# A graph-network kernel whose second layer changes its order of blocks, with a reordered start

## The chip, the cores and the metric

The kernel runs on one core of a Trainium2 chip. The metric is the device time of one execution in microseconds. A profile is one further execution, recorded by the chip's profiler; its span is the time from its first to its last instruction.

## The reference

Two graph layers over 6250 nodes and 200000 edges, all features 128 wide, the edges sorted by receiver `dst`. Cut to what matters:

```python
h = x @ W + b_W; xi, xj = split(h, 2)
m = xj[src] + (edge_attr @ W_e + b_We)
x = layernorm(x + xi + segment_sum(m / (deg[dst] + 1e-6), dst))     # layer 1
h = x @ W1                                                           # layer 2
deg = segment_sum(1, [dst, self]); dinv = rsqrt(deg)
o = segment_sum(h[src] * dinv[src] * dinv[dst], [dst, self]) + b     # with self loops
y = leaky((o - mean) * rsqrt(var + 1e-5) * gamma + beta)             # batch norm over nodes
return layernorm(x + y)
```

## The kernel before

**Blocks and counts.** Receivers are taken in 25 blocks of 256 nodes (the last has 106). For each block the kernel builds a dense matrix of counts, senders by receivers: how many edges run from each sender to each receiver of the block. It is made in 16 slots of 8 pairs of receivers. In each slot VectorE makes two tiles of one-hots (`one_hots`, L509 and L512), TensorE multiplies them (`count`, L737) and ScalarE copies the result to `counts` (`pair_out`, L929). TensorE then gathers by matmuls: `product` (L758) sums x over senders, x being kept as two f16 halves (`xsplit`), so 50 groups of 128 senders make 100 passes of 256 columns.

**The order in one block.** All engines run through blocks b = 0 to 26 and slots s = 0 to 15 in program order. In block b the counts of b are built, the product of b-1 runs, and block u = b-2 gets its end of the first layer: `messages` (sums times weights, s = 1), `offset` and `sums` (VectorE), `root` (ScalarE), `normalise` (VectorE), `z_out` (ScalarE), `z_low` (VectorE). What comes out is z, layer 2's input scaled by 1/sqrt(deg), again as two f16 halves in `zown`. Features of edges are summed by matmuls with one-hots of 32 receivers: `edges` (L777), 2 groups of 4 sets of `EJ` = 10 tiles of 128 edges each, with `edge_one_hots` (L529) from VectorE and 640 KB loads by SyncE.

**The own part of x.** x times (wi + identity) plus a bias is made for all nodes during block 0: `turn_x` (TensorE, 13 groups of transposes), `x_turned` (ScalarE), `own_product` (TensorE, L852), `add_bias` (VectorE, L576). The result lies in the memory that z takes later; `offset` (L583) reads it.

**Starting.** `heads` are every 125th receiver, 1600 numbers, spread to all partitions; VectorE counts in them, GpSimd fetches rows and edges by indirect DMA, and so the start of each block is found. Ahead of block 0 VectorE also prepares the weights (L626 to L630), takes the largest |x| of each row (`largest`, L536) and makes from it a power of two (`scales`) by which x is scaled when it is split (`split_high` on ScalarE, `split_low` on VectorE).

**The second layer.** Block k's product of z can take the senders whose z is ready while the first layer still runs: `early(k)` = 4(k-1) of the 100 passes are made in the first layer (L766) and stored to DRAM. The counts from that point on are stored too (`counts_kept`), except for blocks 23 and 24, which stay in SBUF. After the first layer the blocks are taken in the order `AGAIN`: 0, 23, 24, 1, 2, ..., 22. For the i-th:

- SyncE (in one queue, in this order for each i): `load_counts(i)` (L316) waits for the buffer, gathered i-4; `load_early(i)` (L323) waits for the sums of i-2; `load_inverse(i)` (L329) waits until i-2 is scaled. There are four buffers of counts.
- TensorE: `gather_z(i)` (L818), the 100 - early passes; after the first 20 of them `weights(i-1)` (L835); at the end `add_own(i)` (L827), four matmuls of the block's own z with an identity, for the self loops.
- VectorE: `add_early(i+1)` (L702), then `scale_rows(i)` (L710), then statistics (L695) after ScalarE's bias (`bias_rows`, L1058).

```python
for i in range(NB):                              # VectorE
    if i + 1 < NB and early(AGAIN[i + 1]):
        add_early(i + 1)
    scale_rows(i)
for i in range(1, NB):                           # SyncE
    if i >= 4:
        load_counts(i)
    if early(AGAIN[i]):
        load_early(i)
    if i >= 2:
        load_inverse(i)                          # reach(sp, S["scaled"], i - 1)
```

Last come the batch norm, leaky and the second layer norm (`finish_rows`, lines from L1056 on).

## Time and profile before

| what | value |
|---|---|
| time, median of 3 runs | 1067.37 us (1064.99 to 1072.68) |
| the profiled execution: its time, its span | 1061.45 us, 1059.7 us |
| busy: TensorE, VectorE, ScalarE, GpSimd | 939.2, 700.0, 474.3, 301.6 us |
| mean granted TensorE clock | 0.974 |
| DMA | 249.12 MB, 235 GB/s |

The profile records one execution. "Busy" is the time in which an engine had an instruction in work; PEld is TensorE's weight load, which overlaps PE. In a row of the timeline, what stands in brackets is the engine's idle time before the instruction and what ended it. "SPq" is SyncE's queue issuing a DMA. A span can be cut into stretches, to see which engine is busy in which.

### The profile page before, as it was taken

The numbers are of one execution on the slowest core, as the hardware profiler recorded it, in microseconds if no ns is written. First come the engines' busy times: TensorE is split into PE (matmuls) and PEld (weight loads), VectorE is DVE, ScalarE is ACT, GpSimd is POOL, SyncE is SP. The second block draws the span as 40 slices with busy tenths as digits, with TensorE's granted clock in tenths as the row PEclk, the third lists the DMA queues.
The fourth block names the chain that finished last, engine by engine and source line by source line (L and its number), as shares of the span: only waits on it lengthen the run. The fifth ranks groups of instructions, "written<-read, shape, count | busy, mean of one in ns | idle before, by whom it ended". The sixth has DMA issues, their size and how long they took to land. (4 is left out here: it accounts for less than half of the span.)

```text
span 1059.7 us, 32142 instructions
## 1 busy us (share of the span) xinstructions
PE 939.2 (89%) x12860; PEld 837.3 (79%) x12860; DVE 700.0 (66%) x1728; ACT 474.3 (45%) x932; POOL 301.6 (28%) x389
## 2 busy tenths in 40 slices
PE   2378999998999999999999999999999989887755
PEld 0377888887988988899889888899888778675655
DVE  3978999998998898888888787787511010111256
ACT  1445666665665565565555455455521000000037
POOL 4325655554554333332333323132000000000000
PEclk9899999999999999999999999999999999998878
DMA  7527989899687878787777666666036667665534
GB/s 149 209 106 251 337 328 377 317 350 345 233 321 251 316 249 282 262 283 254 223 243 224 202 227 227 196 193 203 35 153 242 266 240 280 227 217 189 149 102 148
DMA packets 95714, 249.12 MB, mean 235 GB/s; under 512 B 41156, under 2 KB 63384, under 8 KB 90696
## 3 DMA queue, kind: packets, MB, share of 16 engines
q1 hardware_dynamic: 93160, 242.12, 66.3%
q0 software_dynamic: 2400, 4.88, 1.6%
q8 instruction: 104, 1.70, 0.7%
q14 instruction: 50, 0.41, 0.1%
HBM read 192.50 MB, written 54.46 MB: 233 GB/s over the span
## 5 line engine op out<-in xcount | busy, mean ns | idle before, releaser
L929 ACT CAST counts<-pair_ps 128x800 bf16<-128x800 f32 x391 | 319.2, 830 | 301.5 <-PE pair_ps L737 286.9
L509 DVE TENSOR_TENSOR lo_oh<-counter,lo_t 128x1024 bf16<-128x1024 bf16 x391 | 273.5, 700 | 91.3 <-PE pair_ps L737 85.7
L758 PE MATMUL x_ps<-counts,xsplit 128*128 128x256 bf16 (+1 forms) x2500 | 312.6, 271 | 5.9 <-issue 5.8
L758 PEld LDWEIGHTS x_ps<-counts,xsplit 128*128 128x128 f16 x2500 | 227.6, 98 | 37.1 <-issue 14.5
L512 DVE TENSOR_TENSOR key_oh<-counter,key_t 128x800 bf16<-128x800 bf16 x391 | 226.5, 579 | 0.0
L737 PE MATMUL pair_ps<-key_oh,lo_oh 128*128 128x100 bf16 x3128 | 207.0, 208 | 18.6 <-ACT counts L929 6.4
L737 PEld LDWEIGHTS pair_ps<-key_oh,lo_oh 128*128 128x128 bf16 x3128 | 181.7, 98 | 33.1 <-issue 16.2
L766 PE MATMUL x_ps<-counts,zown 128*128 128x256 bf16 (+1 forms) x1104 | 131.5, 268 | 0.0
L777 PE MATMUL e_ps<-streams 128*32 128x128 f32 x3920 | 120.5, 276 | 1.6 <-issue 1.5
L702 DVE TENSOR_TENSOR s_mem<-pair_ps,early_in 128x256 f32<-128x256 f32 (+1 forms) x23 | 9.6, 418 | 160.0 <-PE pair_ps L827 160.0
L777 PEld LDWEIGHTS e_ps<-streams 128*32 128x32 f32 x3920 | 106.3, 111 | 6.8 <-issue 2.7
L766 PEld LDWEIGHTS x_ps<-counts,zown 128*128 128x128 f16 x1104 | 99.8, 98 | 12.4 <-issue 2.6
L818 PE MATMUL pair_ps<-streams,zown 128*128 128x256 bf16 x796 | 93.8, 278 | 17.2 <-DMA streams<-counts_kept 17.2
L818 PEld LDWEIGHTS pair_ps<-streams,zown 128*128 128x128 f16 x796 | 78.8, 100 | 30.5 <-DMA streams<-counts_kept 19.4
L1058 ACT ACTIVATE xsplit<-xsplit,vec 128x256 f32<-128x256 f32 (+1 forms) x25 | 12.6, 505 | 182.0 <-DVE xsplit L710 182.0
L397 POOL TENSOR_SCALAR row_f<-cnt 128x1 f32<-128x1 f32 x25 | 12.8, 512 | 262.7 <-DVE head_junk L462 262.5
L818 PE MATMUL pair_ps<-counts,zown 128*128 128x256 bf16 x600 | 73.2, 282 | 11.4 <-DMA counts<-counts_kept 11.3
L818 PEld LDWEIGHTS pair_ps<-counts,zown 128*128 128x128 f16 x600 | 60.2, 102 | 22.8 <-DMA counts<-counts_kept 13.1
L529 DVE TENSOR_TENSOR streams<-iota,ekeys 128x1280 f32<-128x1280 f32 x49 | 72.9, 1487 | 0.0
L392 POOL DMA_INDIRECT gsrc<-in_src,start_i x25 | 61.9, 2475 | 7.6 <-issue 7.6
L1210 PE MATMUL u_vps<-ident,u_r 128*128 128x128 f32 x100 | 22.5, 310 | 15.5 <-DVE u_r L1191 11.1
L428 POOL TENSOR_SCALAR ein<-ekeys 128x80 f32<-128x80 f32 (+1 forms) x25 | 28.0, 1121 | 22.1 <-DVE ekeys L521 22.1
(158 smaller groups left out, 880.6 us busy)
## 6 DMA issues: line engine op xcount, KB each, us to landing
streams<-in_edge_attr SPq DMA_DIRECT2D x196, 640.0 KB
counts_kept<-counts SPq DMA_DIRECT2D x2, 3200.0 KB
streams<-counts_kept SPq DMA_DIRECT2D x2, 3200.0 KB, 15.3
dinv_row<-dinv_rows SPq DMA_DIRECT2D x25, 128.0 KB, 4.4
edst<-in_dst SPq DMA_DIRECT2D x196, 5.0 KB
counts<-in_x SPq DMA_DIRECT2D x3, 1024.0 KB, 10.2
x_rows<-x_mem SPq DMA_DIRECT2D x24, 128.0 KB
counts_kept<-counts SPq DMA_DIRECT2D x1, 3072.0 KB
```

What stands on the lines that cost most here:

```text
L392: g.indirect_dma_start(out=out, out_offset=None, in_=table, in_offset=bass.IndirectOffsetOnAxis(ap=at, axis=0)).then_inc(done, 16)
L428: step(g.tensor_scalar(ein[:, 0:n], ekeys[:, 0:n], float(EC), None, ALU.is_lt))
L509: dv.tensor_tensor(lo_oh[:, at % RING, :, :, :], counter[:, :, :].unsqueeze(1).to_broadcast([P, SW // 2, P, 2]), pairs(lo_t[b % 2][:, w]). ...
L512: dv.tensor_tensor(key_oh[:, at % RING, :, :, :], counter[:, 0:KW, :].unsqueeze(1).to_broadcast([P, SW // 2, KW, 2]), pairs(key_t[b % 2][: ...
L529: dv.tensor_tensor(e_oh[g][:, :, :], iota[:, 0:EC].unsqueeze(1).to_broadcast([P, EG * EJ, EC]), ekeys[:, k].unsqueeze(2).to_broadcast([P, ...
L737: last = nc.tensor.matmul(pair_ps[at % 2][:, half_of, col:col + KW], lo_oh[:, at % RING, w // 2, :, w % 2], key_oh[:, at % RING, w // 2, : ...
L758: last = nc.tensor.matmul(x_ps[:, 0, 0:n], xsplit[:, q // 2, q % 2, :], by_hi[:, q // 2, :], start=(q == 0), stop=(q == 2 * HI - 1))
L766: last = nc.tensor.matmul(x_ps[:, 1, 0:n], zsplit[:, z // 2, z % 2, :], by_hi[:, z // 2, :], start=(z == 0), stop=(z == early(k) - 1))
L777: last = nc.tensor.matmul(e_ps[EC * c:EC * (c + 1), g, :], e_oh[g][:, c * EJ + j, :], ebuf[g][:, c, j, :], start=(j == 0), stop=(j == EJ - 1))
L818: nc.tensor.matmul(z_ps[i % 2][:, 0:n], zsplit[:, q // 2, q % 2, :], by_hi[:, q // 2, :], start=(q == early(b)), stop=False)
L929: a.copy(out.rearrange("p h (g n) -> p h g n", g=2), pair_ps[at % 2][:, :, 0:4 * KW].rearrange("p g (n h) -> p h g n", h=HI)).then_inc(S[" ...
L1210: nc.tensor.matmul(v_ps[c % VB][:, i, :], r[c % RB][:, base + i % 2:base + BN:2], ident[:, :], start=True, stop=False)
```

## The change

- **Order.** `AGAIN` takes a long and a short block in turn: 0, 23, 24, 1, 22, 2, 21, ..., 11, 12. The half after which `weights` comes is 20 passes or half of the block's, if that is less. Statistics follow where their rows are complete. The loops above stay.
- **Own z.** GpSimd adds an identity to the counts of the block's own 256 senders (`count_itself`), after they have landed (blocks 23 and 24: after their products); the gather waits for it at pass 4b, and the four matmuls of `add_own` go.
- **Nine tiles.** `EJ` is 9 instead of 10, in loads, one-hots and matmuls.
- **Own part of x.** Made block by block: `turn_x(b-1)` (four f16 matmuls from `xsplit`) at s = 3, `x_turned` at s = 4, two products with wi in `messages`; the biases by GpSimd (`add_biases`), `offset` one addition.
- **Start.** 409 heads first; the other 1191 are loaded at the end of block 0 and spread in block 1. `largest` stands before and between the first starts of blocks, `scales` and the weights after the first slots' one-hots, the splitting of x at slots 3 to 12 of block 0. Edge matmuls of block 0 come later (s = 9, 14).
- **Later steps.** `root` at s = 7 (5), `normalise` 12 (9), the rows 12 and z 13 (8), `z_low` in the next block's s = 3 (12).

```diff
-EK, EG, EJ, EC, EP = 8, 4, 10, 32, 16
+EK, EG, EJ, EC, EP = 8, 4, 9, 32, 16
-AGAIN = [0, NB - 2, NB - 1] + list(range(1, NB - 2))
+AGAIN = [0, NB - 2, NB - 1] + [b for k in range(1, NB // 2) for b in (k, NB - 2 - k)]
...
+            def add_biases(b):
+                pool.wait_ge(S["weights_ready"], 1)
+                reach(pool, S["offset_ready"], b)
+                for t in range(2):
+                    last = g.tensor_scalar(bias[:, t, :], bje, share[:, 2 * b + t:2 * b + t + 1], None, ALU.mult)
+                step(last)
+                g.tensor_tensor(bias[:, :, :], bias[:, :, :], bi.unsqueeze(1).to_broadcast([P, 2, F]),
+                                ALU.add).then_inc(S["bias_ready"], 1)
+
+            def count_itself(i):
+                b = AGAIN[i]
+                n = cols(b)
+                if b < NB - 2 or i == 0:
+                    pool.wait_ge(counts_in[i % 4], 16 * again_loads(i))
+                else:
+                    pool.wait_ge(S["product_done"], b + 1)
+                    pool.wait_ge(S["early_done"], early_blocks(b + 1))
+                by_hi = again[AGAIN_AT[i % 4]][:, 0:HI * n].rearrange("p (h n) -> p h n", n=n)[:, 2 * b:2 * b + 2, :]
+                g.tensor_tensor(by_hi, by_hi, itself[:, :, 0:n], ALU.add).then_inc(S["itself_counted"], 1)
...
             def offset(u):
-                dve.wait_ge(S["shares_ready"], u + 1)
-                dve.wait_ge(S["own_added"], len(OWN))
-                for t in range(2):
-                    last = dv.scalar_tensor_tensor(out=vo[:, t, :], in0=bje,
-                                                   scalar=share[:, 2 * u + t:2 * u + t + 1],
-                                                   in1=own[:, 2 * u + t, :], op0=ALU.mult, op1=ALU.add)
-                last.then_inc(S["offset_ready"], 1)
+                dve.wait_ge(S["messages"], u + 1)
+                dve.wait_ge(S["bias_ready"], u + 1)
+                dv.tensor_tensor(vo[:, :, :], j_ps[:, 2:4, :], bias[:, :, :], ALU.add)\
+                  .then_inc(S["offset_ready"], 1)
...
             make_keys(0)
-            largest()
-            scales()
-            invert_degrees(0)
             for b in range(NB + 2):
                 u = b - 2
                 for s in range(SL):
                     if b < NB and s < slots(b):
                         one_hots(b, s)
                     if b == 0:
-                        if s in LOW_AT:
-                            split_low(LOW_AT.index(s))
+                        if s == 0:
+                            scales()
+                        if s == 1:
+                            spread_scales()
+                            ready_weights()
...
+                for t in range(2):
+                    nc.tensor.matmul(j_ps[:, 2 + t, :], xT[:, t, :], wi, start=True, stop=True)
...
-                    nc.tensor.matmul(z_ps[i % 2][:, 0:n], zsplit[:, q // 2, q % 2, :], by_hi[:, q // 2, :],
-                                     start=(q == early(b)), stop=False)
-
-            def add_own(i):
...
+                    if q == 4 * b:
+                        pe.wait_ge(S["itself_counted"], i + 1)
+                    last = nc.tensor.matmul(z_ps[i % 2][:, 0:n], zsplit[:, q // 2, q % 2, :], by_hi[:, q // 2, :],
+                                            start=(q == early(b)), stop=(q == 2 * HI - 1))
+                    if q == 2 * HI - 1:
+                        last.then_inc(S["z_gathered"], 1)
...
+            def turn_x(k):
+                reach(pe, S["xT_out"], k)
+                reach(pe, S["tabled"], min(k + 2, NB))
+                pe.wait_ge(S["ident16_ready"], 1)
+                for t in range(2):
+                    for q in range(2):
+                        last = nc.tensor.matmul(keys_ps[:, 2 + t, :], xsplit[:, 2 * k + t, q, :], ident16[:, :],
+                                                start=(q == 0), stop=(q == 1))
                 last.then_inc(S["x_turned"], 1)
...
+            def float_far_heads():
+                act.wait_ge(S["heads_in"], 32)
+                a.copy(heads_sb[0:1, NEAR:R], heads_sb[0:1, NEAR:R].bitcast(I32)).then_inc(S["far_heads_float"], 1)
```

## Rows read from the trace of the kernel before

**Rows 1.** Section 1 of the page: busy time, share of the span, instructions.

```profile
PE 939.2 (89%) x12860; PEld 837.3 (79%) x12860; DVE 700.0 (66%) x1728; ACT 474.3 (45%) x932; POOL 301.6 (28%) x389
```

**Rows 2.** Busy time, granted clock and DMA in stretches from the start to the second layer.

```profile
core 0: us, PE busy (x) PEld busy (x) DVE busy (x) ACT busy (x) POOL busy (x), PEclk, DMA share, GB/s
0.00:34.77 34.77, 7.68 (x13) 3.19 (x13) 15.78 (x50) 6.27 (x11) 12.32 (x32) 1.00 0.73 176
34.77:85.28 50.51, 34.96 (x435) 32.16 (x436) 39.67 (x78) 24.78 (x36) 13.36 (x18) 0.90 0.38 138
85.28:108.83 23.55, 19.91 (x356) 17.11 (x354) 23.10 (x53) 12.40 (x20) 16.99 (x15) 1.00 0.82 297
...
588.10:620.90 32.80, 32.34 (x478) 28.98 (x476) 25.22 (x60) 17.08 (x34) 10.42 (x15) 1.00 0.64 210
795.94:1012.10 216.16, 184.51 (x1550) 157.04 (x1547) 30.60 (x88) 15.76 (x36) 0.00 (x0) 0.96 0.63 220
```

**Rows 3.** Timeline ahead of block 0: start, duration, engine, line, op.

```profile
18.32 0.34 DVE L469 TENSOR_SCALAR_CACHE_REDUCE row_junk<-rows,th 128x125 bf16<-128x125 int32 x1 [6.32 <-DMA rows<-in_dst,row_i]
...
25.12 6.94 DVE L536 TENSOR_REDUCE rowmax<-counts 128x16 f32<-128x2048 f32 x3
...
25.96 0.27 ACT L959 CAST lo_t<-keys_ps 128x128 bf16<-128x128 f32 x1
```

**Rows 4.** Groups of instructions by line and shape: busy, mean ns, idle before.

```profile
L777 PE MATMUL e_ps<-streams 128*32 128x128 f32 x3920 | 120.5, 276 | 1.6 <-issue 1.5
...
L529 DVE TENSOR_TENSOR streams<-iota,ekeys 128x1280 f32<-128x1280 f32 x49 | 72.9, 1487 | 0.0
...
L583 DVE SCALAR_TENSOR_TENSOR vo<-linear,share,zown 128x128 f32<-128x128 f32 x50 | 15.1, 341 | 0.0
...
L827 PE MATMUL pair_ps<-ident,zown 128*128 128x128 f16 x96 | 14.5, 305 | 0.0
...
L702 DVE TENSOR_TENSOR s_mem<-pair_ps,early_in 128x256 f32<-128x256 f32 x22 | 9.3, 425 | 160.0 <-PE pair_ps L827 160.0
...
L576 DVE TENSOR_TENSOR zown<-j_ps,linear 128x512 f32<-128x512 f32 x12 | 8.3, 689 | 6.3 <-PE j_ps L852 6.3
...
L852 PE MATMUL j_ps<-linear,x_mem 128*128 128x128 f32 x52 | 7.7, 292 | 5.2 <-DVE zown L576 4.9
```

**Rows 5.** Timeline of the second layer, gathers of blocks 4, 5 and 6.

```profile
859.81 0.60 PE L827 MATMUL pair_ps<-ident,zown 128*128 128x128 f16 x4
...
860.20 2.39 PE L818 MATMUL pair_ps<-streams,zown 128*128 128x256 bf16 x20
...
860.79 0.41 DVE L710 TENSOR_TENSOR xsplit<-pair_ps,dinv_row 128x256 f32<-128x256 f32 x1
...
861.64 0.38 SPq L316 DMA_DIRECT2D streams<-counts_kept  x1
...
869.85 0.60 PE L827 MATMUL pair_ps<-ident,zown 128*128 128x128 f16 x4
...
872.56 2.36 PE L818 MATMUL pair_ps<-streams,zown 128*128 128x256 bf16 x20 [2.11 <-DMA streams<-counts_kept]
```

**Rows 6.** Timeline of the second layer, a gather after a longer wait.

```profile
957.33 4.02 PE L818 MATMUL pair_ps<-counts,zown 128*128 128x256 bf16 x20 [2.43 <-DMA counts<-counts_kept]
```

**Rows 7.** DMA issues: size of each, us from issue to landing.

```profile
streams<-counts_kept SPq DMA_DIRECT2D x1, 3072.0 KB, 12.6
...
counts<-counts_kept SPq DMA_DIRECT2D x1, 2816.0 KB, 11.5
...
streams<-counts_kept SPq DMA_DIRECT2D x1, 2560.0 KB, 10.9
...
counts<-counts_kept SPq DMA_DIRECT2D x1, 1920.0 KB, 9.9
```

**Rows 8.** Timeline of GpSimd: one add at each of two widths.

```profile
93.88 0.39 POOL L429 TENSOR_TENSOR eacc<-eacc,ein 128x80 f32<-128x80 f32 x1
...
755.27 0.27 POOL L429 TENSOR_TENSOR eacc<-eacc,ein 128x40 f32<-128x40 f32 x1
```

More of the change, by code:

```diff
@@ L51 @@
 X_PIECES = ((0, 8), (8, 16), (16, NB))
-OWN = [(h, min(4, HI - h)) for h in range(0, HI, 4)]
-OWN_LAG = 5
-LOW_AT = (4, 8, 12)
+HIGH_AT, LOW_AT, HEADS_AT = (3, 5, 8), (6, 9, 12), (9, 11, 13)
 CHUNK_ENDS = (1, 3, 7, 11, 15, 19, 22, 24, NB)
 CHUNKS = list(zip((0,) + CHUNK_ENDS, CHUNK_ENDS))
-AGAIN = [0, NB - 2, NB - 1] + list(range(1, NB - 2))
+AGAIN = [0, NB - 2, NB - 1] + [b for k in range(1, NB // 2) for b in (k, NB - 2 - k)]
 AGAIN_AT = (2, 0, 1, 3)
@@ L105, in early_blocks, with segments @@
     return sum(early(j) > 0 for j in range(k))
+def segments(i):
+    ready = lambda k, j: all(b in AGAIN[:j] for b in range(k * SEG // BN, (k * SEG + SEG - 1) // BN + 1))
+    return [k for k in range(NB) if ready(k, i + 1) and not ready(k, i)]
 def again_loads(i):
@@ L450, in _ @@
                     windows(b + 2)
+                if b >= 1:
+                    add_biases(b - 1)
+            add_biases(NB - 1)
+            pool.wait_ge(S["built"], first_slot(NB - 1) + slots(NB - 1))
+            step(g.memset(itself[:, :, :], 0.0))
+            for t in range(2):
+                last = g.tensor_copy(itself[:, t, t:BN:2], ident[:, :])
+            step(last)
+            for i in range(NB):
+                count_itself(i)
         @block.vector
@@ L655, in _ @@
                         edge_one_hots(b, 0)
-                    if s == 7 and b + 1 < NB:
+                    if s == (7 if b else 10) and b + 1 < NB:
                         invert_degrees(b + 1)
@@ L669, in _ @@
                         start_of(b + 3)
-                    if s == 9 and 0 <= u < NB:
+                    if s == 12 and 0 <= u < NB:
                         normalise(u)
@@ L673, in _ @@
                         edge_one_hots(b, 1)
-                    if s == 12 and 0 <= u < NB:
-                        z_low(u)
-                if b == 0:
-                    for m in range(SL - OWN_LAG, len(OWN)):
-                        add_bias(m)
+                    if s == 3 and 1 <= u <= NB:
+                        z_low(u - 1)
+            z_low(NB - 1)
             for k, n in enumerate((E, E, P * HI, P)):
@@ L817, in gather_z @@
                         pe.wait_ge(S["z_low"], NB)
-                    nc.tensor.matmul(z_ps[i % 2][:, 0:n], zsplit[:, q // 2, q % 2, :], by_hi[:, q // 2, :],
-                                     start=(q == early(b)), stop=False)
-            def add_own(i):
-                b = AGAIN[i]
-                n = cols(b)
-                pe.wait_ge(S["ident16_ready"], 1)
-                for t in range(2):
-                    for q in range(2):
-                        last = nc.tensor.matmul(z_ps[i % 2][:, t:n:2], zsplit[:, 2 * b + t, q, :], ident16[:, 0:n // 2],
-                                                start=False, stop=(t == 1 and q == 1))
-                last.then_inc(S["z_gathered"], 1)
+                    if q == 4 * b:
[4 more added lines that the diff above has]
+                        last.then_inc(S["z_gathered"], 1)
             def weights(i):
@@ L855, in _, with spread_far_heads @@
+            def spread_far_heads(k):
+                pe.wait_ge(S["far_heads_float"], 1)
+                pe.wait_ge(S["scale_ready"], 1)
+                reach(pe, S["far_heads_spread"], k)
+                at = NEAR + FAR_PIECE * k
+                nc.tensor.matmul(far_ps, ones[0:1, :], heads_sb[0:1, at:at + FAR_PIECE], start=True, stop=True)\
+                  .then_inc(S["heads_broadcast"], 1)
             pe.wait_ge(S["heads_float"], 1)
             pe.wait_ge(S["consts"], 2)
-            nc.tensor.matmul(heads_ps[0], ones[0:1, :], heads[0:1, 0:HEAD_PIECE], start=True, stop=True)\
+            nc.tensor.matmul(heads_ps, ones[0:1, :], heads[0:1, :], start=True, stop=True)\
@@ L858, in _ @@
               .then_inc(S["heads_broadcast"], 1)
-            pe.wait_ge(S["heads_rest_float"], 1)
-            for k in range(1, R // HEAD_PIECE):
-                nc.tensor.matmul(heads_ps[k], ones[0:1, :], heads[0:1, HEAD_PIECE * k:HEAD_PIECE * (k + 1)],
-                                 start=True, stop=True).then_inc(S["heads_broadcast"], 1)
             pe.wait_ge(S["consts"], 5)
-            turn_keys(0)
             pe.wait_ge(S["pmax_ready"], 1)
             nc.tensor.transpose(few_ps[0:1, 0, 0:P], pmax[:, :], ident[:, :]).then_inc(S["pmax_out"], 1)
-            pe.wait_ge(S["few_ready"], 1)
@@ L868, in _ @@
-            nc.tensor.matmul(few_ps[:, 1, 0:4], ones[0:1, :], few[0:1, :].bitcast(F32), start=True, stop=True)\
-              .then_inc(S["few_out"], 1)
-            pe.wait_ge(S["weights_ready"], 1)
-            for k, (a, z) in enumerate(X_PIECES):
-                pe.wait_ge(S["x_in"][k], 16 if z < NB else 32)
+            turn_keys(0)
             for b in range(NB + 2):
@@ L905, in _ @@
                 first = early(AGAIN[i])
-                half = min(first + 20, 2 * HI)
+                half = first + min(20, (2 * HI - first) // 2)
                 gather_z(i, first, half)
```

202 lines of the change are left out of this document (98 added, 104 removed).

## The prediction

> **What bounds the kernel now.** I read the page's shares first: TensorE is busy 89% of the span and nothing else comes near it [rows 1]. That is an average, so I cut the span into stretches [rows 2], at the starts of the one-hots of blocks 0, 1 and 19, at the first gather of the second layer and at its last statistics. There the limits differ.
>
> Up to 34.77 us no count matmul runs: VectorE works towards block 0's keys and the scale of x. Block 0 then takes 50.51 us, where block 1 takes 23.55 and has VectorE busy for 23.10 of them: block 0 pays for the own part of x and the splitting of x. Block 19 is TensorE's (32.34 of 32.80). The blocks in between grow with the early passes, and I put the change from one limit to the other at block 7. The second layer takes 216.16 us with TensorE busy for 184.51.
>
> The second layer is where the change's main edit lies, and its busy share misleads. One step in the timeline [rows 5]: the gather of block 4 ends with its own-z matmuls at 859.81; VectorE adds the early sums of block 4 and only then scales block 3 (860.79); SyncE, whose queue holds the inverse-degree load that waits for that scaling, issues the next counts at 861.64; those are for block 6, and the gather of block 6 starts only at 872.56, after 2.11 us of waiting for them. The gather of block 5 (860.20 to 869.85) is all that lies in between. So although there are four buffers, a load goes out when the gather two places before its own has ended, and is covered by exactly one gather, the one just before its own. In ascending order that gather is about as long as the load: load 10.9 us, gather 9.65.
>
> **The change part by part.** Start: the row maxima (6.94 us [rows 3]) and the scale chain leave the path. The first two maxima fall where VectorE waits for the rows of receivers (6.32 us of idle in front of the first row count [rows 3]); the third (2.5) takes the place of the weights' preparation. The first one-hots waited for the scale only; without it they start when the tables are ready (26.23 [rows 3]), about 26.5 instead of 34.77: -8.2 us. Fewer head elements are loaded ahead of x; I count nothing for that.
>
> Block 0: VectorE was busy for 39.67 us of it. Thirteen additions of the own part go (12 of 0.69 and a short one [rows 4], 8.7), scales and weights come in (about 4.0), nine tiles instead of ten take 10% off two edge one-hots of 1.49: 0.3. That leaves 34.7; with some 2 us of waiting for ScalarE's high halves and for DMA, 37 instead of 50.51: -13.5. The ping-pong of TensorE, ScalarE and VectorE over the own part, which made the idle in this block, is gone. The bound on the one side is 34.7, on the other 42.
>
> Blocks 1 to 6, VectorE's: edge one-hots -0.3, the offset from two ops of 0.34 to one of the kind that takes 0.43 [rows 4], -0.26. Block 1 gets the far heads: three broadcasts on TensorE and three copies and a 1.2 us conversion on ScalarE, both with slack; their load is queued behind the second edge group, and if it comes late ScalarE stops with all copies behind it (0 to 3 us). GpSimd's bias work (three ops a block) has room, since it idles on the heads' count, but may slow VectorE a little. Sum: -2 us, -4 to +2.
>
> Blocks 7 to 25, TensorE's: edge matmuls cost 120.5/49 = 2.46 us a group, two groups, a tenth off: -0.49. The own product now runs here, four records at 7.7/52 = 0.148: +0.59, or +0.46 in a dense stretch; the turning of x by four f16 matmuls is like the four of the own z: +0.60 at most, +0.40 as the following gather starts 0.40 after them. Net +0.4 to +0.7 a block, 19 blocks: +8, where TensorE has nothing to hide it behind. The later root, scaling and low half of z only take waits off ScalarE and VectorE; what the product needs of them is still a dozen slots early. At the end of the layer the chain to the last low half of z grows by about 1 us; only the last 4 of the 100 passes of the second layer's first gather need it, so the other 96 (10.5 us) hide it.
>
> First layer together: -8.2 - 13.5 - 2 + 8 = -16 us (-26 to -8).
>
> Second layer, order: the pairs are (1,22), (2,21) ... (11,12). By the step above a long load is now covered by a short gather and a short load by a long gather. TensorE and the DMA engines take turns. For each long block from 3 to 11 the cycle is: 1.3 us from the end of the previous long gather to the issue; the landing; the long gather; then the next. The short gather lies inside the landing and saves nothing. Landings by size go from 11.5 us (88 passes) over 10.9 (80) to 9.9 (60) [rows 7], in sum about 94.5 for the nine. The nine gathers are 684 passes of 0.1092 = 74.7, and 0.45 each for the weights' product, 4.0. Issue delays 9 x 1.3 = 11.7. The stall in front of each is 4 to 9 us (landing + 1.3 - short gather of 3 to 6), and after a wait of 2.43 us 20 passes took 4.02 us instead of 2.36 [rows 5, 6]: the granted clock had dropped to the lower of the two levels, half of the full one. Nine times 1.5: 13.5.
>
> Own z by the counts: four matmuls a block go (0.4 us for the four), but on the path only in the long steps. In their place GpSimd adds to 2 x 256 bf16 after the landing, and TensorE waits for it at its fifth pass, 0.44 us into a gather at full clock, 0.85 at the lower. The trace has no such op. The nearest: an add over 40 elements takes 0.27 us, one over 80 takes 0.39 [rows 8], so 3 ns an element, 1.7 us for 512. Bounds: 0.4 (as 80 elements) and 2.3. With 1.7 the wait is 0.9 in each long step: 8 us. Short blocks have landed long before, and their addition is done.
>
> The Trainium skill (GPSIMD Engine Reference, "Performance versus the Vector engine") gives 2.6 cycles at 1.2 GHz for each element of a two-input op, 1.1 us plus dispatch, as an estimate for these 512; by it the wait would be 0.4 a step and the sum 4 us less. [...]
>
> The sum: block 2's load goes out with the first ones, at about 814, lands after 12.6 [rows 7], and its gather takes 10.5 and 2.4 of the same additions: it ends at 839. Then 94.5 + 74.7 + 4.0 + 11.7 + 13.5 + 8 = 206.4, to 1045; the last short gather (56 passes, 6.6) and the tail of 3.4 as now: 1055. Landings should be a little quicker where a load has the queue to itself, so I take 1053 against 1012.1 before: +41 us (+24 to +55). The batch norm and the final rows, the 47.6 us from 1012.1 to the end of the span, stay.
>
> Total: -16 + 41 = +25 on the profiled execution's 1061.45 (span 1059.7 and 1.8 around it), 1086. The median of the runs shown is 6 us above that execution, so the median after should lie between 1086 and 1092: **1088 us**.
>
> **The rivals.** Near-null: the front gains what it can (-26) and the pairs lose less (+22: landings near 9 us with the queue to themselves, GpSimd's addition at its lower bound, clock drops half as long): about 1064. For it: landings of the same size scatter by 1 us. Against: it needs every term at its end.
>
> Faster: the loads do run ahead. The mechanism is the ring of four; if a long load goes out before the preceding long gather ends, it is covered, and the second layer becomes pure TensorE: 1276 passes x 0.1092 and the weights' products, some 149 us from block 1's start at about 811, and the tail: 964, -48; with the front -64, about 1003. It decides at one point: whether SyncE gets past the inverse-degree load while the long gather runs. For it: the buffers are free, and GpSimd or SyncE hold no other wait. Against: every issue in the trace comes 0.85 us after a scaling that stands behind the next block's early sums, and nothing in the diff touches that.
>
> Slower still: the addition costs over 2.5 us, the lower clock lasts through a gather's first 5 us after idle times of 9 us (longer than any in the second layer's trace), or the far heads stop ScalarE: 1112 and over.
>
> Not doing what it says: nine tiles hold 1152 edges for 32 receivers; counted in the reference's inputs, the fullest group has 1104. If it overflowed, the general path would take many times as long. I give it nothing.
>
> **How the numbers follow.** Forecast (pairs serialised, 1070 to 1110): 0.66. Near-null, 1057 to 1070: 0.16. Loads run ahead, below 1057: 0.09. Slower still, over 1110: 0.09. The range takes in the near-null case: 1059 to 1111. A measurement of this kernel tells about 1% (10.7 us) from no change. Slower by over 1% (above 1078): 0.72; within: 0.18; faster: 0.10.
>
> **What would show it.** Right: the first one-hots near 26.5; block 1 starting near 63; late blocks 0.4 us longer; in the second layer waits of TensorE for the counts of 4 to 9 us, nine times, each in front of a long block, none in front of a short one, with 20 passes at the lower clock after each; DMA and TensorE busy in turn; the layer taking 250 to 260 us. Wrong: counts of block k+1 issued before block k's gather ended; waits under 2 us; TensorE busy for most of the second layer. The front is wrong if block 0 stays above 42 us or block 1 has ScalarE waiting for the far heads.

## The result, and the profile after

The changed kernel takes 1096.01 us (median of 4 runs, 1092.80 to 1101.56), the kernel before beside it 1070.03 us (1064.99 to 1074.58): the ratio is 1.025, interval 1.018 to 1.032. A second measurement (the last experiment) gave 1074.28 against 1049.61 us, ratio 1.0244, interval 1.0197 to 1.0291. So the change makes the kernel 2.5% slower, 25 us.

The profiled execution took 1101.56 us. The shares of its page answer to [rows 1]; the engines' lines give busy time, share of the span and instructions:

```profile
span 1099.7 us, 31421 instructions
PE 937.2 (85%) x12418; PEld 821.6 (75%) x12418; DVE 688.9 (63%) x1690; ACT 468.5 (43%) x944; POOL 354.5 (32%) x492
```

TensorE was busy for as long as before (939.2), with 442 matmuls fewer, and the span grew by 40.0 us. So the new time is mostly waiting, and part of the busy time is now at a lower clock (0.946 in the mean instead of 0.974). The windows answer to [rows 2]: block 0, block 1, blocks 15 to 23 together, and the second layer from its first gather to its last statistics.

```profile
24.85:59.63 34.78, 15.86 (x200) 12.26 (x204) 34.32 (x79) 19.43 (x24) 19.08 (x18) 0.95 0.60 212
59.63:88.47 28.84, 26.41 (x420) 21.92 (x417) 23.76 (x53) 14.18 (x24) 13.21 (x18) 0.89 0.62 192
444.44:739.15 294.71, 286.08 (x4139) 256.08 (x4138) 222.93 (x511) 154.46 (x307) 100.81 (x152) 0.99 0.60 193
787.37:1051.19 263.82, 187.38 (x1448) 151.54 (x1448) 30.71 (x88) 15.70 (x36) 26.86 (x24) 0.84 0.49 177
```

The start and block 0 gained what they should: the first one-hots at 24.85 us instead of 34.77, block 0 in 34.78 instead of 50.51, VectorE busy for 34.32 of it. But the first gather came at 787.37 instead of 795.94, so of these 25.6 us only 8.6 were left: blocks 1 to 24 had given 17 back. The second layer took 263.82 instead of 216.16 us, with TensorE's busy time 3 us longer for 102 matmuls fewer, and both the granted clock (0.84 for 0.96) and the DMA share (0.49 for 0.63) down. Neither TensorE nor the DMA engines are the bound there: they work in turn.

The waits of TensorE in the second layer: what it waited for, in total, how often, the longest.

```profile
PE pair_ps L856 <- DMA streams<-counts_kept: 38.0, 5, 10.6
PE pair_ps L856 <- DMA counts<-counts_kept: 32.8, 5, 9.5
PE pair_ps L856 <- POOL streams L455: 1.5, 6, 0.6
```

Ten waits of any size for counts, 70.8 us, one in front of each long block from 2 to 11 and none in front of a short one. One step of the timeline, which answers to [rows 5] and [rows 6]:

```profile
845.53 1.03 PE L856 MATMUL pair_ps<-streams,zown 128*128 128x256 bf16 x4 [10.63 <-DMA streams<-counts_kept]
845.55 1.15 POOL L455 TENSOR_TENSOR streams<-streams,key_oh 128x512 bf16<-128x512 bf16 x1 [21.91 <-DMA streams<-counts_kept]
846.76 3.60 PE L856 MATMUL pair_ps<-streams,zown 128*128 128x256 bf16 x16 [0.20 <-POOL streams L455]
...
851.00 9.48 PE L856 MATMUL pair_ps<-streams,zown 128*128 128x256 bf16 x84
...
859.21 0.42 DVE L740 TENSOR_TENSOR s_mem<-pair_ps,early_in 128x256 f32<-128x256 f32 x1 [22.53 <-PE pair_ps L856]
859.55 0.41 DVE L748 TENSOR_TENSOR xsplit<-pair_ps,dinv_row 128x256 f32<-128x256 f32 x1
860.00 0.32 SPq L339 DMA_DIRECT2D dinv_row<-dinv_rows  x1
...
860.41 0.38 SPq L326 DMA_DIRECT2D counts<-counts_kept  x1
...
860.75 1.47 PE L856 MATMUL pair_ps<-streams,zown 128*128 128x256 bf16 x12
...
871.74 1.04 PE L856 MATMUL pair_ps<-counts,zown 128*128 128x256 bf16 x4 [9.51 <-DMA counts<-counts_kept]
```

The long gather of block 3 runs from 845.53 to 859.17. Only when it is over does VectorE add its early sums (859.21) and then scale the rows of the block before it (859.55); SyncE's inverse-degree load follows (860.00), and behind it in the same queue the counts of block 4 (860.41). All that is left to cover their landing is the short gather, whose second half stands at 860.75. It ends at 862.22, and TensorE waits until 871.74. The first 20 passes after a wait took 1.03 + 3.60 us, where 20 take 2.2 at full clock.

### The profile page after: what moved, and what is told of

Its sections match the earlier page's. It is cut to its first block and busy times, and to the rows that moved or that the text cites. A ratio compares the mean times of both kernels' runs of the same rounds, so it can differ in the third digit from the quotient of the medians.

```text
span 1099.7 us, 31421 instructions
## 1 busy us (share of the span) xinstructions
PE 937.2 (85%) x12418; PEld 821.6 (75%) x12418; DVE 688.9 (63%) x1690; ACT 468.5 (43%) x944; POOL 354.5 (32%) x492
## 5 line engine op out<-in xcount | busy, mean ns | idle before, releaser
L554 DVE TENSOR_TENSOR key_oh<-counter,key_t 128x800 bf16<-128x800 bf16 x391 | 230.0, 588 | 0.0
L856 PE MATMUL pair_ps<-streams,zown 128*128 128x256 bf16 x796 | 100.7, 289 | 39.5 <-DMA streams<-counts_kept 38.0
L856 PEld LDWEIGHTS pair_ps<-streams,zown 128*128 128x128 f16 x796 | 81.3, 103 | 58.2 <-DMA streams<-counts_kept 39.4
L807 PE MATMUL e_ps<-streams 128*32 128x128 f32 x3528 | 114.1, 278 | 5.8 <-issue 5.8
L807 PEld LDWEIGHTS e_ps<-streams 128*32 128x32 f32 x3528 | 96.4, 111 | 14.2 <-issue 9.8
L856 PE MATMUL pair_ps<-counts,zown 128*128 128x256 bf16 x600 | 77.4, 291 | 34.2 <-DMA counts<-counts_kept 32.8
L571 DVE TENSOR_TENSOR streams<-iota,ekeys 128x1152 f32<-128x1152 f32 x49 | 68.5, 1398 | 0.0
L441 POOL TENSOR_SCALAR bias<-linear,share 128x128 f32<-128x128 f32 x50 | 53.6, 1081 | 28.5 <-DVE vo L630 27.6
L455 POOL TENSOR_TENSOR streams<-streams,key_oh 128x512 bf16<-128x512 bf16 x13 | 15.0, 1151 | 132.9 <-DMA streams<-counts_kept 132.9
L455 POOL TENSOR_TENSOR counts<-counts,key_oh 128x512 bf16<-128x512 bf16 (+1 forms) x12 | 13.2, 1107 | 100.3 <-DMA counts<-counts_kept 100.3
```

The source lines that it names most:

```text
L441: last = g.tensor_scalar(bias[:, t, :], bje, share[:, 2 * b + t:2 * b + t + 1], None, ALU.mult)
L455: g.tensor_tensor(by_hi, by_hi, itself[:, :, 0:n], ALU.add).then_inc(S["itself_counted"], 1)
L554: dv.tensor_tensor(key_oh[:, at % RING, :, :, :], counter[:, 0:KW, :].unsqueeze(1).to_broadcast([P, SW // 2, KW, 2]), pairs(key_t[b % 2][: ...
L571: dv.tensor_tensor(e_oh[g][:, :, :], iota[:, 0:EC].unsqueeze(1).to_broadcast([P, EG * EJ, EC]), ekeys[:, k].unsqueeze(2).to_broadcast([P, ...
L807: last = nc.tensor.matmul(e_ps[EC * c:EC * (c + 1), g, :], e_oh[g][:, c * EJ + j, :], ebuf[g][:, c, j, :], start=(j == 0), stop=(j == EJ - 1))
L856: last = nc.tensor.matmul(z_ps[i % 2][:, 0:n], zsplit[:, q // 2, q % 2, :], by_hi[:, q // 2, :], start=(q == early(b)), stop=(q == 2 * HI ...
```

## The experiments

Times are medians. The first four kernels ran on one chip (before: 1061.67 us), the other eight on another (before: 1051.07 and 1049.61 us). The chips differ by 1%, so ratios to before are compared across chips, and stretches of a profile only with those of the same chip where a few us matter. For the same reason the times expected from the fifth kernel on, which go by the first chip's, are read through the ratios: 1% of them is the chip. The record doesn't say on which chip the first pair of profiles (before and change) was taken.

| kernel | us | ratio to before, interval | first gather at | second layer |
|---|---|---|---|---|
| old order | 1059.92 | 0.997, 0.993 to 1.001 | 780.4 | 221.3 |
| order alone | 1101.72 | 1.038, 1.033 to 1.043 | 787.0 | 264.2 |
| run ahead by two | 1001.29 | 0.942, 0.938 to 0.947 | 784.5 | 169.7 |
| the same, old order | 1007.36 | 0.948, 0.943 to 0.953 | 784.2 | 174.7 |
| before, run ahead by two | 1017.44 | 0.966, 0.961 to 0.971 | 784.5 | 185.0 |
| run ahead by one | 986.17 | 0.937, 0.932 to 0.941 | 765.3 | 171.7 |
| run ahead by two, ten tiles | 998.03 | 0.947, 0.942 to 0.952 | 784.3 | 168.0 |
| run ahead by two, x turned twice | 985.21 | 0.936, 0.930 to 0.941 | 769.5 | 168.4 |
| run ahead by one, heads by GpSimd | 988.35 | 0.941, 0.936 to 0.946 | 770.6 | 173.4 |
| run ahead by two, own z by matmuls | 989.91 | 0.943, 0.939 to 0.947 | 770.0 | 177.4 |
| run ahead by one, own product twice | 994.62 | 0.949, 0.944 to 0.953 | 772.8 | 172.2 |
| the change again | 1074.28 | 1.024, 1.020 to 1.029 | 764.2 | 262.0 |

**Is it the order?** The changed kernel with the old order:

```diff
-AGAIN = [0, NB - 2, NB - 1] + [b for k in range(1, NB // 2) for b in (k, NB - 2 - k)]
+AGAIN = [0, NB - 2, NB - 1] + list(range(1, NB - 2))
```

> The changed kernel with only the order of the second layer's blocks put back to ascending; own z by the counts' diagonal, nine tiles, own x block by block and the new prologue stay. Theory (the pairs cost the time: each long load is covered by a short gather alone): the second layer goes back to about 218 us with 2 to 3 us of waiting per block, the long waits of 5 to 10 us are gone, and the whole takes about 1052 us (1045 to 1058), so some 1.5 to 2% under the kernel before. Rival (the diagonal addition on GpSimd, or the lower clock, makes the second layer long whatever the order): 1085 to 1100 us, the second layer still over 245 us.

```profile
780.36:1001.70 221.34, 182.22 (x1448) 148.20 (x1448) 30.73 (x88) 15.69 (x36) 26.87 (x24) 0.92 0.59 211
```

Its second layer is 42.5 us shorter, and the long waits are gone. The total is 8 us above what I expected (1052, 1045 to 1058) and level with the kernel before. The profile can't account for these 8 us, since the profiled execution took 1051.5, where I had expected it; the ten executions lie between 1048.7 and 1065.2. What it does show is a small gain: the first gather comes only 6.6 us earlier than in the next kernel, which has the old first layer on the same chip, and the second layer is 5.2 us longer than that of before [rows 2]. TensorE there waits 5.7 us in all for GpSimd's additions (3.2 and 2.5, 14 waits), and the clock is lower (0.92 for 0.96).

The kernel before with the new order alone (and the statistics in the order in which their rows become complete):

```diff
-AGAIN = [0, NB - 2, NB - 1] + list(range(1, NB - 2))
+AGAIN = [0, NB - 2, NB - 1] + [b for k in range(1, NB // 2) for b in (k, NB - 2 - k)]
...
-                half = min(first + 20, 2 * HI)
+                half = first + min(20, (2 * HI - first) // 2)
```

> The kernel before with only the order of the second layer's blocks changed to long and short in turn (and the two formulas that follow from it: which segments' statistics are ready, and where the early passes are halved). Theory: the second layer grows from 216 to about 255 to 264 us, the first layer stays, in all 1110 to 1118 us, 4 to 4.5% over the kernel before, more than the whole change cost, because the faster start is missing. Rival (the edits work only together, the order alone is harmless): 1070 us, within 1%.

```profile
786.97:1051.16 264.19, 196.70 (x1550) 164.17 (x1547) 30.57 (x88) 15.68 (x36) 0.00 (x0) 0.87 0.50 180
```

The second layer grows by 48.0 us and the kernel by 3.8%, a little less than the 4 to 4.5% expected. The order is the whole loss, and it is there without GpSimd's addition (0.00 for POOL).

**Is it bandwidth or the place in the queue?** The changed kernel with one edit in SyncE's loop:

```diff
-                if i >= 4:
-                    load_counts(i)
+                if 4 <= i + 2 < NB:
+                    load_counts(i + 2)
```

> The changed kernel with one edit on SyncE: in the second layer's loop the counts of block i+2 are issued where those of block i were, ahead of the two loads whose buffers wait for VectorE, so that a load goes out two gathers earlier. Theory (not bandwidth but the place in SyncE's queue sets when the loads start): the waits of 5 to 10 us in front of the long blocks vanish, the second layer falls from 264 to some 165 to 185 us, the whole to 1010 to 1025 us. Rival 1 (the DMA engines are the bound): 1080 to 1100 us, DMA engines busy above 80% in the second layer. Rival 2 (the own z on GpSimd or the chain over VectorE is next): between, 1035 to 1060 us, with TensorE's waits moved to the addition of the diagonal or to the early sums.

> As the run-ahead kernel, but with the blocks in ascending order. If loads that run ahead leave TensorE as the only bound, the order no longer matters: 1010 to 1025 us, within 0.5% of the same edit in the order of pairs. Rival (the pairs do buy something once loads run ahead, since in ascending order the long gathers come last and the long loads together, ahead of the buffers): 10 to 20 us slower than in pairs. Rival 2 (DMA-bound): both at about 1050 to 1100.

The windows of the first of the two, and below them the second's:

```profile
784.45:954.14 169.69, 164.52 (x1448) 143.67 (x1448) 30.64 (x88) 15.70 (x36) 26.89 (x24) 1.00 0.77 276
```

```profile
784.18:958.89 174.71, 165.51 (x1448) 144.68 (x1448) 30.75 (x88) 15.69 (x36) 26.88 (x24) 0.98 0.76 267
```

All waits for counts are gone, TensorE is busy for 164.5 of 169.7 us at full clock, and the same bytes land in two thirds of the time: 276 GB/s where the change had 177. The loss was the place in the queue, not the DMA engines. Of the 94 us by which this layer is shorter than the change's, 71 are the waits for counts, and 23 are TensorE's busy time: the same 1448 matmuls take 164.5 us at full clock and took 187.4 at 0.84. The total falls below my range for it (1001.3 for 1010 to 1025). The old order then costs 5.0 us of the layer; its one long wait says where:

```profile
PE pair_ps L865 <- DVE s_mem L740: 7.0, 3, 6.0
```

In the run-ahead kernel in pairs this line has 2.8 us in 4 waits, 1.3 at most. TensorE's weights' product waits once for 6.0 us for the early sums. Why these came late there was not followed up; the early sums' load now stands behind counts that wait for their buffer. Both expectations for the order missed, the first narrowly: the totals differ by 6.1 us, where one said at most 0.5% (5 us) and the other 10 to 20.

The same edit in the kernel before, and a run-ahead of one place (i + 1) in the changed kernel:

> The kernel before with the run-ahead edit alone: SyncE issues the counts of block i+2 at the place where it issued those of block i. The old order, the old start, ten tiles and the own z by matmuls stay. Theory: what the run-ahead edit gives, it gives without the change too: the second layer falls from 216 to about 176 us, the whole to 1018 to 1025 us. The distance to the run-ahead kernel in the old order (1007 us) is then what the first layer's edits are worth, 10 to 18 us. Rival (the own z by the counts' diagonal is what lets TensorE run through, since four matmuls and an addition by GpSimd leave its path): 1030 us or more.

> The changed kernel with the counts of block i+1 issued where those of block i were: one place of run-ahead instead of two. A load then goes out one gather earlier and is covered by a long and a short gather together, 13 to 16 us, which is more than the 12 us that the longest landing takes. Theory: nearly all of the gain of two places is there, 1001 to 1012 us, with waits of at most 1 to 2 us in front of the first long blocks. Rival (the gain comes from the depth of two): 1030 to 1060 us, waits of 3 to 5 us in front of each long block.

```profile
784.54:969.52 184.98, 177.25 (x1550) 155.82 (x1547) 30.71 (x88) 15.69 (x36) 0.00 (x0) 0.98 0.72 257
```

```profile
765.29:936.97 171.68, 164.94 (x1448) 142.56 (x1448) 30.68 (x88) 15.69 (x36) 26.83 (x24) 1.00 0.77 272
```

The edit helps the kernel before too (0.966), its layer falling to 185.0 rather than the 176 I expected. One place of run-ahead nearly suffices: 171.7 us, with 0.7 us of waiting for counts in all (its total, 0.937 of before and so some 994 us by the first chip's times, is below the 1001 to 1012 expected), and its three profiles in the table (171.7, 173.4, 172.2) stand 3 to 5 us above those of two places on the same chip (168.0, 168.4). Against the kernel before with the same run-ahead, the rest of the change is worth 1.8% in the old order (0.948 for 0.966), 2.4% in pairs (0.942).

**What do the small terms cost?** Three kernels undo or double one term where TensorE is the bound: ten tiles (EJ = 10) and the turning of x done twice on the run-ahead by two, the own product done twice on the run-ahead by one.

```diff
                 for t in range(2):
+                    for q in range(2):
+                        nc.tensor.matmul(keys_ps[:, 2 + t, :], xsplit[:, 2 * k + t, q, :], ident16[:, :],
+                                         start=(q == 0), stop=(q == 1))
+                for t in range(2):
                     for q in range(2):
...
-                for t in range(2):
+                for t in (0, 1, 0, 1):
                     nc.tensor.matmul(j_ps[:, 2 + t, :], xT[:, t, :], wi, start=True, stop=True)
```

> The run-ahead kernel with ten edge tiles a group instead of nine. By the prediction's rows: 0.49 us more of TensorE in each block that it bounds (7 to 24: +9) and 0.3 us of VectorE in the others (+2): 1012 us, 1.1% over the run-ahead kernel (1001). Rival (the edge work lies beside other work, as the late blocks grew by 0.53 us although it fell): within 0.3%.

> The run-ahead kernel with the four matmuls that turn a block's own x done twice (the first set of four is overwritten by the second, so the result stays). Prices the own part of x block by block: 0.4 to 0.6 us in each block that TensorE bounds, 25 blocks in all, so +8 to +12 us: 1009 to 1013 us. Rival (the turning fills a gap of TensorE, and the late blocks' +0.53 us came from elsewhere): within 3 us of 1001.

> The one-ahead kernel with the two own products of a block done twice (the second overwrites the first with the same numbers). The prediction's price of the own product is 0.46 to 0.59 us in each block that TensorE bounds: +8 to +11 us in blocks 7 to 24, and less before. Rival (as with the turning of x, done twice for 0.17 us a block, it costs a third of its row): +3 us.

Blocks 7 to 23, from the first one-hot of block 7 to that of block 24, took 503.2 us in the one-ahead kernel on this chip (213.87 to 717.09), 512.6 with ten tiles, 506.2 with x turned twice and 508.9 with the own product twice. Over 17 blocks that is 0.55, 0.17 and 0.33 us each. But a mean over this stretch is a poor price: blocks 19 to 22 of one and the same first layer took 128.5 to 129.6 us in four executions on this chip. Blocks 8 to 18 together repeat within 0.1 us in all of them. Block 16 by windows: the kernel before with run-ahead, then the one-ahead kernel, ten tiles, x turned twice and the own product twice.

```profile
489.67:519.47 29.80, 29.12 (x455) 26.52 (x453) 25.11 (x60) 16.91 (x34) 10.42 (x15) 1.00 0.75 244
464.44:494.46 30.02, 29.34 (x447) 26.70 (x445) 24.98 (x59) 16.95 (x35) 12.33 (x18) 1.00 0.68 224
479.01:509.46 30.45, 29.77 (x463) 27.13 (x461) 25.37 (x59) 17.05 (x35) 11.45 (x18) 1.00 0.71 238
467.96:498.21 30.25, 29.57 (x451) 26.95 (x449) 25.25 (x58) 17.07 (x35) 13.36 (x18) 1.00 0.69 223
469.65:500.12 30.47, 29.80 (x451) 27.16 (x449) 25.10 (x59) 17.05 (x35) 11.64 (x18) 1.00 0.66 221
```

So a block that TensorE bounds pays 0.43 for the tenth tile, 0.23 for turning x and 0.45 for the own product, and the other blocks from 8 to 18 give the same within 0.04. The whole change costs such a block 0.22 us (30.02 for 29.80; 0.21 to 0.23 in blocks 14 to 18), and the three prices add up to it: 0.23 + 0.45 - 0.43 = 0.25. The totals on this chip agree for the own product (994.6 for 986.2 us).

Ten tiles cost more in blocks 2 to 6, where I had put 0.3 us a block: 135.7 us for 127.0. Block 3, by windows, of the kernel with ten tiles and of the one with nine:

```profile
113.34:141.75 28.41, 24.94 (x409) 22.49 (x408) 25.02 (x59) 16.45 (x34) 19.95 (x20) 0.97 1.01 379
```

```profile
112.24:136.85 24.61, 24.29 (x398) 21.70 (x396) 24.61 (x58) 16.65 (x34) 17.84 (x18) 1.00 0.92 334
```

VectorE's busy time differs by 0.4 us only, the block's by 3.8. With ten tiles the DMA share is 1.01, and TensorE has gaps for which the trace shows no wait, 2.7 us in one place. Edges read by DMA would fit this, since they are what ten tiles add for that resource. Against it stands block 4 of the kernel before with run-ahead: ten tiles too, a DMA share of 1.03, and 24.6 us. The cause stays open. The totals of the first two can't be set against their parent: x turned twice stands at 0.936, no slower than its parent on the other chip (0.942), for with the new first layer the late blocks on that chip were long, as will be seen.

Own z put back to matmuls, without the addition, on the run-ahead by two:

```diff
-                    if q == 4 * b:
-                        pe.wait_ge(S["itself_counted"], i + 1)
...
+            def add_own(i):
...
+                for t in range(2):
+                    for q in range(2):
+                        last = nc.tensor.matmul(z_ps[i % 2][:, t:n:2], zsplit[:, 2 * b + t, q, :],
+                                                ident16[:, 0:n // 2], start=False, stop=(t == 1 and q == 1))
...
```

> The run-ahead kernel (two places) with the own z of the second layer put back to four matmuls a block, and without GpSimd's addition to the counts. By the prediction's row (0.4 us for the four) and since TensorE now bounds the layer: +10 us, the second layer 180 instead of 170 us. Rival (the addition on GpSimd costs TensorE as much, by waits at its fifth pass or by slower counts): 168 to 173 us.

```profile
769.95:947.34 177.39, 174.15 (x1550) 154.17 (x1547) 31.11 (x89) 15.69 (x36) 0.00 (x0) 1.00 0.73 265
```

177.4 against 168.0 and 168.4: the diagonal saves 9 us once TensorE is the bound. With the loads late it cost 5 (old order). It is the same edit; what stands beside it decides its sign. This also accounts for the 185.0 us of the kernel before with run-ahead: 15.3 more than the changed one's 169.7, of which the old order is 5.0 and the own z by matmuls 9.

**Why is block 1 long?** In the three profiles with the old first layer block 1 took 23.5 us, in the eleven with the new one 26.7 to 33.0. GpSimd in ScalarE's place for the far heads, on the run-ahead by one:

```diff
-HIGH_AT, LOW_AT, HEADS_AT = (3, 5, 8), (6, 9, 12), (9, 11, 13)
+HIGH_AT, LOW_AT, HEADS_AT = (3, 5, 8), (6, 9, 12), (10, 12, 14)
...
+                if b == 1:
+                    pool.wait_ge(S["heads_in"], 32)
+                    g.tensor_copy(heads_sb[0:1, NEAR:R], heads_sb[0:1, NEAR:R].bitcast(I32))\
+                     .then_inc(S["far_heads_float"], 1)
...
-                    if b == 1 and s == HEADS_AT[0] - 1:
-                        float_far_heads()
```

> The one-ahead kernel with the far heads turned into floats by GpSimd (in block 1, before its bias work) instead of by ScalarE, and their three broadcasts one slot later. In the changed kernel's block 1 ScalarE spends 1.18 us on that conversion with the copies of two count slots behind it, TensorE waits 1.18 us for it, and VectorE waits 3.1 us at the block's end. Theory (this is why block 1 takes 27 to 29 us instead of the 23.5 of before): block 1 falls by 1.2 to 2.5 us, the whole by about 2 us against the one-ahead kernel (984 to 986 on a like chip, ratio to before 0.933 to 0.937). Rival (the three broadcasts and the late edge group fill TensorE anyway, or GpSimd is late with its windows): block 1 unchanged at 27 us.

```profile
PE j_ps L887 <- POOL heads_sb L485: 5.4, 1, 5.4
```

A miss: GpSimd came to the conversion at 82.0 us, TensorE waited 5.4 us for it, and block 1 took 31.5. The kernel with own z by matmuls gives better evidence. Its first layer is the change's own, and yet block 1 took 33.0 us there, against 26.7 when the change ran again on the same chip. First what TensorE waited for, then the window:

```profile
PE j_ps L886 <- ACT heads_sb L1036: 2.1, 1, 2.1
```

```profile
59.47:92.48 33.01, 29.75 (x420) 23.96 (x417) 23.91 (x53) 14.36 (x24) 12.98 (x18) 0.79 0.59 183
```

The same window when the change ran again, where the longest wait for the heads is 0.9 us:

```profile
59.44:86.14 26.70, 24.37 (x420) 20.79 (x417) 23.56 (x54) 14.17 (x24) 13.18 (x18) 0.95 0.61 192
```

In the 33.0 us block ScalarE had waited 1.1 us for the heads' DMA, issued at 65.6 and in at 78.8. VectorE's work is the same in both (23.9 and 23.6 us), so the 6.3 us come from 1.2 us more of waiting for the heads and from what follows: the granted clock at 0.79 instead of 0.95, TensorE busy 5.4 us longer for the same matmuls. The block in two stretches shows when the clock fell:

```profile
63.25:80.32 17.07, 13.80 (x229) 12.36 (x226) 16.96 (x38) 11.11 (x19) 11.89 (x16) 1.00 0.55 154
80.32:90.56 10.24, 10.24 (x94) 6.79 (x97) 3.17 (x6) 2.44 (x4) 0.00 (x0) 0.50 0.87 282
```

TensorE had idled for 2.07 us until 80.05; from 80.32 the granted clock was half the full one for 10.24 us in which TensorE never stopped. In the eleven profiles the clock fell a second time in block 1 in three, the three longest: this one, the one with GpSimd (31.5 us) and the change's first (28.8, after a wait of 1.18 us). In the other eight it did not, and they took 26.7 to 27.6. The length of the wait alone doesn't decide it, for the old-order kernel waited 1.59 us without a fall. The 3.2 us by which even the shortest exceeds the old 23.5 are not shown term by term; these blocks begin with 1.1 to 4.1 us at the lower clock, where the old one ran at full clock throughout, and TensorE waits 0.9 us or more for the heads.

**Do the late blocks grow?** The change once more, with nothing edited:

> The changed kernel once more, beside the three others on one chip. Its blocks 15 to 23 took 294.7 us in the first profile, those of the same code in the one-ahead kernel 282.6, and its TensorE stood idle there for no wait that the trace shows, 5.8 us in 16 places inside the edge matmuls. If that belongs to the chip or the execution, blocks 15 to 23 take the same here in all kernels with this first layer, whichever of the two it is; if it belongs to what the change puts behind them, this kernel alone shows 292 or more. The ratio to before should again be 1.02 to 1.03, or 1.01 to 1.02 where the late blocks are short.

Blocks 15 to 23 took 282.3 us here, as in the five other kernels with nine tiles on this chip (282.4 to 284.6), and 292.7 to 294.8 in the change's first profile and the three with nine tiles from the first chip. What differs is one line. The first profile of the change, and this one, TensorE by lines over blocks 15 to 23 (busy us, mean ns of one, idle before):

```profile
L788 PE MATMUL x_ps<-counts,xsplit 128*128 128x256 bf16 x900 | 113.9, 275 | 0.8 <-issue 0.7
...
L770 PE MATMUL pair_ps<-key_oh,lo_oh 128*128 128x100 bf16 x1152 | 75.4, 208 | 1.9 <-issue 1.9
L807 PE MATMUL e_ps<-streams 128*32 128x128 f32 x1296 | 44.3, 274 | 5.8 <-issue 5.8
```

```profile
L788 PE MATMUL x_ps<-counts,xsplit 128*128 128x256 bf16 x900 | 112.6, 273 | 1.0 <-issue 0.8
...
L770 PE MATMUL pair_ps<-key_oh,lo_oh 128*128 128x100 bf16 x1152 | 75.1, 208 | 1.9 <-ACT counts L951 1.9
...
L807 PE MATMUL e_ps<-streams 128*32 128x128 f32 x1296 | 39.1, 274 | 0.0
```

Counts and products cost the same; the edge matmuls took 50.1 us with their gaps instead of 39.1, 11.0 of the 12.4 us. It belongs to the chip or the execution, not to what stands behind it. The order-alone kernel, with ten tiles and the old first layer, had no such gaps on the first of the two chips (281.4 us), so it isn't the chip alone either.

## Why the prediction was right

It gave 1088 us and 1059 to 1111; 1096.0 came, 26.0 us over before where +21 stood. By its steps:

**The start and block 0: right.** First one-hots at 24.85 (26.5), block 0 in 34.8 (37), VectorE's busy time 34.32 (34.7).

**Blocks 1 to 6: the term that failed.** They were to gain 2 us and lost 5.8 in the first profile (154.0 to 159.8). Block 1 alone lost 5.3. The prediction gave TensorE and ScalarE slack for the far heads and put a price (0 to 3 us) only on a late load. In the change's first profile the load was not late, and TensorE still waited 1.18 us for the conversion, after which the clock fell for 3.4 us. Where the load was late, by 1.1 us (own z by matmuls), block 1 took 9.5 us more than the old one. The lower clock is what the term left out. Blocks 2 to 6, on like chips, went from 129.3 to 126.6.

**Blocks 7 to 23: +8 predicted, +9.0 measured, and the agreement is chance.** The kernel before with run-ahead and the change, on one chip, took 501.3 and 503.0 us there: +1.7. In a block that repeats, the change costs 0.22 us, where the sum had +0.4 to +0.7. The nine tiles gave 0.43 (0.49) and the own product cost 0.45 (0.46 to 0.59), both nearly as priced; the turning of x cost 0.23 (0.40 to 0.60), about half of its price by records at their full length. And three earlier blocks (7, 11 and 13) were 0.8 to 1.3 us shorter than before, so that blocks 7 to 13 took 192.0 us for 194.2. The rest of the 9.0 in the first profiles is two disturbances that partly cancel. Beside the two later profiles, the change's first was longer by 16.7 us (12.4 of them in blocks 15 to 23, mostly the edge matmuls' gaps), and that of before by 9.4 (6.6 of them in blocks 7 to 14, for a cause not followed up).

**First layer together: -16 predicted.** The first pair of profiles shows -8.6; on one chip it is 784.5 against 764.2, -20.4. Both lie in the range given (-26 to -8), the first at its end.

**The second layer: the mechanism was right in each link, the size 5 to 7 us short.** +41 predicted, +47.7 measured; the layer's 263.8 us are outside the 250 to 260 named as a sign, and the longest wait was 10.6 us where 4 to 9 were named. The nine long steps, from the trace of the change: landings 95.2 us (94.5); issue delays 1.24 each, 11.1 (11.7); the nine gathers from first pass to last 102.2. Of these 74.7 are passes at full clock, 4.0 weights' products, 1.8 waits for GpSimd (8); the 21.7 left are the lower clock (13.5). So the clock cost 2.4 us a step instead of 1.5, if the whole remainder is put down to it. The row that I had [rows 6] already said 1.66 (4.02 - 2.36); the first 20 passes took 4.3 us in the mean (2.2 at full clock), and in five of the nine steps the weights' product took 0.98 to 1.06 us instead of 0.60, which I had left out. Longer waits did not make it worse: after the wait of 9.51 us the 20 passes took 4.0 us, after that of 6.96 they took 4.6. GpSimd cost 0.2 instead of 0.9, since its addition took 1.15 us (1.7) while TensorE's first four passes ran slowly. These two errors nearly cancelled. Then block 2's gather ended 44.9 us after the first gather began, not 43.1, and the 2 us that I took off for quicker landings were not there: landings were no quicker with the queue to themselves.

By the Trainium skill (GPSIMD Engine Reference, "Performance versus the Vector engine"), 2.6 cycles an element, the estimate for that addition was 1.1 us; the measured 1.15 us agrees with it, and is nearer than the 1.7 that I drew from the rows of 40 and 80 elements.

**The rivals.** The faster one, loads that run ahead, did not happen in this change, and its point of decision was put rightly: SyncE has to get past the inverse-degree load while the long gather runs. Given that by an edit, the kernel takes 1001.3 us where the rival said 1003, with a second layer of 169.7 us where the rival's sum has 168 (795.9 to 964, on the time axis of before). The near-null case had its term in the front (-20 on one chip), but the second layer was far from its +22.

## What to carry over

- Where loads wait in an in-order queue behind a small load that depends on the last engine of the chain, buffers don't make a prefetch. Find for each load the event that lets it out, and count what runs between that and its use; an order of long and short blocks then matters only because that cover is one block. Moving the load one place ahead in the queue took 8% off the changed kernel (986.2 for 1074.3 us on one chip), which then stood 6.3% under the kernel before.
- A price for an added instruction depends on the neighbour: the same diagonal addition cost 5 us where loads were late and saved 9 where TensorE was the bound. Fix the bound first, then judge the small edits.
- A total that comes out as predicted does not show that its terms did. Two profiles of the same code differed here by 12 us in nine blocks. Take the price of a small term from blocks that repeat from profile to profile, not from a sum over blocks that don't: by the sum over 17 blocks the own product cost 0.33 us a block, by the blocks that repeat 0.45.

## What was not expected of the hardware

- The same instructions on the same data took 39.1 us in one execution and 44.3 with 5.8 us of gaps in another, all in the edge matmuls, with no wait in the trace. In the first profile it is, in six of the nine blocks, the first edge group, which took 2.8 to 4.8 us instead of 2.2. It came in the change's first profile and all three with nine tiles on the first chip, in none of the six on the second, and not with ten tiles on the first. The cause stays open.
- Landings of counts overlap well. Run ahead, with two or three loads under way at once, the layer moved 276 GB/s in the mean where the change moved 177, and a single landing took only 1.1 us longer: the nine long loads took 105.4 us in sum from issue to landing, against 95.2.
- A load of 1191 scattered elements of 4 bytes (the far heads, in the kernel with own z by matmuls), issued at 65.6 us, landed at 78.8, 13 us later, beside the edges' traffic; in the change's two profiles it had landed before ScalarE asked for it at 77 to 78 us.
